# Grouping the value products of an attention kernel two blocks of keys at a time

## What is computed

```python
q, k = _apply_rope(q, cos, sin), _apply_rope(k, cos, sin)
scores = jnp.einsum('bhqd,bhkd->bhqk', q, k) / jnp.sqrt(jnp.float32(dh))
scores = jnp.where(causal[None, None, :, :], scores, -jnp.inf)
attn = jax.nn.softmax(scores, axis=-1)
out = jnp.einsum('bhqk,bhkd->bhqd', attn, v)
```

## Time and profile before

| | us |
|---|---|
| median of 3 runs (1317.09 to 1321.57) | 1317.52 |
| the profiled execution | 1314.68 |
| its span, first to last instruction | 1312.8 |
| TensorE busy | 1207.6 (92%) |
| VectorE busy | 732.1 (56%) |
| GpSimd busy | 696.6 (53%) |
| ScalarE busy | 486.5 (37%) |
| mean granted TensorE clock | 0.967 |

### The profile page before, as it was taken

How to read it: one execution, slowest core, us unless ns; L and a number is a source line. 1 busy time by engine, 2 the same in 40 slices (tenths; PEclk the granted TensorE clock), 3 DMA queues, 4 the chain that set the end, 5 groups by cost and what they waited for, 6 DMA issues and landing times.

```text
span 1312.8 us, 25609 instructions
## 1 busy us (share of the span) xinstructions
PE 1207.6 (92%) x8264; PEld 1000.3 (76%) x8264; DVE 732.1 (56%) x1512; ACT 486.5 (37%) x988; POOL 696.6 (53%) x984
## 2 busy tenths in 40 slices
PE   3799999999999999978999999999999999999950
PEld 3466666666666666568899999999999999999950
DVE  5777787878777876665334433343433334333554
ACT  2145454545454545533333323333322333322310
POOL 4234335353535351577567655576665566752675
PEclk9599999999999999989999999999999999999985
DMA  5776745454545455441321121131211222101366
GB/s 135 208 235 178 228 103 169 101 165 103 165 102 163 104 151 110 149 150 44 113 65 59 57 70 65 64 104 57 66 61 62 94 77 66 56 29 34 103 206 234
DMA packets 83100, 147.85 MB, mean 113 GB/s; under 512 B 9647, under 2 KB 60728, under 8 KB 78910
## 3 DMA queue, kind: packets, MB, share of 16 engines
q1 hardware_dynamic: 65344, 111.37, 29.7%
q0 software_dynamic: 7936, 26.60, 5.9%
q10 hardware_dynamic: 9728, 8.67, 2.1%
HBM read 93.05 MB, written 53.61 MB: 112 GB/s over the span
## 4 chain that ended last, share of the span: by engine, by line
PE 48%; POOL 1%; DVE 1%; issue 1%; DMA 0%; POOLq 0%; DVEq 0%
PE ps L77 47%; PE ps L1266 1%; DVE raw L1429 1%; POOL wf_hi L1546 1%; POOL wg_hi L1546 1%; DMA wg_hi<-slot_outputs,slot_all 0%; POOLq L1574 0%; POOL wp_lo L1546 0%; DVE al L1419 0%; DVE ah L1410 0%; DVE xl L1334 0%; DVEq L1574 0%; POOLq L1546 0%; DVE o_sb L1444 0%; DVE gated L1457 0%
## 5 line engine op out<-in xcount | busy, mean ns | idle before, releaser
L1493 POOL TENSOR_TENSOR al<-hid,ah 128x384 fp32r<-128x384 f32 (+1 forms) x176 | 187.4, 1065 | 232.7 <-DVE ah L1410 232.7
L1362 ACT ACTIVATE fc<-ps,b_fc 128x384 f32<-128x384 f32 (+1 forms) x192 | 115.6, 602 | 451.1 <-PE ps L77 451.1
L1457 DVE SCALAR_TENSOR_TENSOR gated<-ps,b_gate,fc 128x384 f32<-128x384 f32 (+1 forms) x192 | 123.4, 642 | 236.9 <-PE ps L77 226.4
L796 DVE TENSOR_REDUCE mx<-ps 128x2 f32<-128x256 f32 (+3 forms) x256 | 205.7, 818 | 39.0 <-PE ps L411 37.5
L411 PE MATMUL ps<-kst,qst 65*128 65x256 f32 (+2 forms) x512 | 149.8, 376 | 0.0
L579 ACT ACTIVATE probs<-ps 128x512 f32<-128x512 f32 (+1 forms) x256 | 125.3, 542 | 60.8 <-PE ps L437 59.8
L1444 DVE TENSOR_TENSOR o_sb<-ps,b_proj 128x256 f32<-128x256 f32 x80 | 33.9, 424 | 176.5 <-PE ps L77 176.5
L571 ACT ACTIVATE probs<-ps 128x256 f32<-128x256 f32 (+1 forms) x128 | 62.6, 490 | 151.6 <-PE ps L428 151.1
L937 POOL TENSOR_TENSOR rope_c<-qk_b,rope_table 128x512 f32<-128x512 f32 x32 | 42.6, 1330 | 128.1 <-ACT qk_b L607 128.0
L77 PE MATMUL ps<-xl,wg_hi 128*128 128x384 f32 (+1 forms) x384 | 103.1, 350 | 1.7 <-issue 1.7
L437 PE MATMUL ps<-qst,kst 66*128 66x512 f32 (+1 forms) x256 | 103.5, 448 | 0.0
(11 more groups left out here) (181 smaller groups left out, 2540.0 us busy)
## 6 DMA issues: line engine op xcount, KB each, us to landing
qk_parts<-hilo SPq DMA_DIRECT2D x32, 512.0 KB, 2.8
qst<-qk_parts SPq DMA_DIRECT2D x64, 256.0 KB, 4.8
kst<-qk_parts SPq DMA_DIRECT2D x64, 256.0 KB, 5.2
slot_tokens<-zeros POOLq DMA_DIRECT2D x12, 816.0 KB, 6.4
rows<-slot_tokens SPq DMA_DIRECT2D x24, 384.0 KB, 3.8
slot_outputs<-o_sb SPq DMA_DIRECT2D x72, 128.0 KB, 1.7
raw<-in_wf SPq DMA_DIRECT2D x8, 1024.0 KB, 5.2
raw<-in_wg SPq DMA_DIRECT2D x8, 1024.0 KB, 7.4
```

What stands on the lines that cost most here:

```text
L796: V.reduce_max(mx[:, g % 2, 2 * pr:2 * pr + 2, i], both[:, :, 0:P * (i + 1)], AXX)\
L1362: A(fc[:, hc % 2, 0:width], ps[:, FC + hc % 2, 0:width], ACT.Identity, bias=b_fc[:, e, hc:hc + 1]).then_inc(fc_out, 1)
L1457: V.scalar_tensor_tensor(gated[:, hc % 2, 0:width], ps[:, GATE + hc % 2, 0:width], b_gate[:, e, hc:hc + 1], fc[:, hc % 2, 0:width], ALU.ad ...
L1493: G.tensor_tensor(al[:, at, 0:width], hid[:, hc % 2, 0:width], ah[:, at, 0:width].bitcast(F32), ALU.subtract).then_inc(al_done, 1)
```

## The change

The tile of probabilities with two buffers becomes four tiles, one for each block of keys, each as wide as that block's queries. In slot 5 the value products of blocks 0 and 1 follow one another, in slot 1 of the next step those of blocks 2 and 3. ScalarE's wait before it writes block j is now for the product of block j of the step before.

```diff
-        probs = sb("probs", [P, 2, GH, T])
+        probs = [sb(f"probs{j}", [P, GH, T - P * j]) for j in range(TT)]
...
-                    last = mm(pvb[32 * h:32 * h + 32, P * j:T], v_sb[:, j, GH * g + h, :], probs[:, j % 2, h, P * j:T],
+                    last = mm(pvb[32 * h:32 * h + 32, P * j:T], v_sb[:, j, GH * g + h, :], probs[j][:, h, :],
                               start=(j == 0), stop=(j == TT - 1))
...
-                        if u in (3, 5, 7) and (not isinstance(b, int) or 0 <= s - 2 <= 31):
-                            pv(s - 2, b - (g < 2), (g - 2) % 4, (u - 3) // 2)
+                        if u == 5 and (not isinstance(b, int) or 0 <= s - 2 <= 31):
+                            pv(s - 2, b - (g < 2), (g - 2) % 4, 0)
+                            pv(s - 2, b - (g < 2), (g - 2) % 4, 1)
                         if u == 1 and (not isinstance(b, int) or 0 <= s - 3 <= 31):
+                            pv(s - 3, b - (g < 3), (g - 3) % 4, 2)
                             pv(s - 3, b - (g < 3), (g - 3) % 4, 3)
...
-                        wait(act, pv_done, 4 * t + j - 1)
-                    A(probs[:, j % 2, 2 * pr:2 * pr + 2, P * j:T],
+                        wait(act, pv_done, 4 * t + j - 3)
+                    A(probs[j][:, 2 * pr:2 * pr + 2, :],
...
-                        wait(act, pv_done, 4 * t + j - 1)
-                    A(probs[:, j % 2, 2 * pr + hh, P * j:T], ps[:, S2 + hh, P * j - q0:T - q0], ACT.Exp,
+                        wait(act, pv_done, 4 * t + j - 3)
+                    A(probs[j][:, 2 * pr + hh, :], ps[:, S2 + hh, P * j - q0:T - q0], ACT.Exp,
```

## The result

The changed kernel takes 1333.34 us (1331.37 to 1334.00, 4 runs), the kernel before 1317.3 in the same comparison: ratio 1.0113, 95% interval 1.0088 to 1.0137. It is slower, as forecast. It lies within the range for 8 in 10 (1312 to 1335), just outside the forecast's own (1321 to 1333), and 6 us above the number: 16 us more than before, where 9.5 were forecast. The profiled execution has a span of 1329.5 us for 1312.8, at a mean granted clock of 0.955 for 0.967.

A forecast was written before the change was run, and what follows sets the result against it. TensorE was taken to bound the attention loop; +8.5 us for batches 2 to 6, +1.0 for batch 1 and 0 for the outer batches gave +9.5, a median of 1327.0 us (own range 1321 to 1333, 8 in 10: 1312 to 1335).

The forecast's parts named there:

- the joins: Two value groups run together, sparing a change of array shape: 0.18 us each, 0.36 a step, 11.4 over 32 steps.
- Rival (d): At the pairs, joining saves nothing because the array empties between accumulations anyway: 11.4 us not saved, 1338 us; chance 0.04.
- Tiles, waits, ScalarE at nothing: Probability tiles (20 KB a partition for 16), looser waits and ScalarE's exponentials add 0, at most 0.1 us a batch either way.
- The cover: Value groups leaving slots 3 and 7 had filled TensorE's waits for VectorE; moving them makes a loop batch 1.7 us longer.
- the four waits: New TensorE waits: 0.7 us at xn's second transposes, 0.9 step 1's projection, about 2 step 2's slot 4, 0.9 the maxima.
- the walk: Following TensorE's lateness slot by slot through one loop batch's four steps: +1.7 us a batch, 8.5 for batches 2 to 6.
- the 0.66 of slot 7: Time freed when the third value group leaves slot 7, 0.66 us; at the maxima it gains nothing before step 3.
- Rival (a): In the attention loop cover doesn't matter, only saved shape changes count: -11.4 us, 1306.1 us; chance 0.13.
- Rival (b): Losses at the projection (0.82) and the maxima (0.66) are half as large: +5.3 us, 1323 us; chance 0.16.
- the 0.82 of the walk: Loss at step 1's slot 4 projection, which waits for VectorE's division: -0.24 instead of -1.06, 0.82 us, six times.
- The lock: VectorE and GpSimd share ports exclusively; 1.85 us of the copy of v waits for GpSimd's addition, order kept.
- Rival (c): The copy of v goes before GpSimd's addition; six batches give back 1.85 us each, 11.1 us: -1.6, 1316 us; chance 0.09.

The follow-up runs named there:

- 11: Changed kernel with the first pair behind slot 3's attention transposes (slot 5 in step 0), the second in slot 0 before the maxima's transpose: 1310.7 us, ratio 0.9949.
- experiment 1: Changed kernel's four tiles and looser ScalarE waits, but all value products in their old slots as in the kernel before: 1318.3 us, ratio 1.0008.
- experiment 3: Changed kernel with only the second pair joined (blocks 2 and 3 in slot 1), blocks 0 and 1 alone in slots 3 and 5: 1323.5 us, ratio 1.0044.
- 2: Changed kernel with only the first pair joined (blocks 0 and 1 in slot 5), block 2 in slot 7, block 3 in slot 1: 1327.7 us, ratio 1.0068.
- experiment 5: Changed kernel with 20 extra matmuls, result thrown away, in TensorE's wait at slot 4 of step 2: 1331.8 us, ratio 1.0105.
- 8: Changed kernel with GpSimd's addition of bias to residual waiting until VectorE's copy of v is done: 1335.5 us, ratio 1.0125.
- experiment 9: Kernel before with GpSimd's addition of bias to residual waiting until VectorE's copy of v is done: 1322.1 us, ratio 1.0033.
- experiment 6: Changed kernel with GpSimd's addition moved from slot 1 to slot 7 of step 2, away from the copy of v: 1341.3 us, ratio 1.0174.
- 7: Kernel before with GpSimd's addition moved from slot 1 to slot 7 of step 2, away from the copy of v: 1345.6 us, ratio 1.0216.
- experiment 4: Changed kernel, but in step 2 block 0 stays in slot 3 and block 1 stands alone in slot 5: 1326.7 us, ratio 1.0044.
- 12: Kernel of 11 with GpSimd's addition also waiting until VectorE's copy of v is done: 1312.4 us, ratio 0.9961.

## Why the prediction was right, and where its size was off

**Bound and saving.** TensorE was the bound, and the joins save what was worked out and a little more. A joined pair lasts 1.64 us against 1.00 + 0.78 and one entry of 0.09, so each join gives 0.23, not 0.18. With the pairs at better places (11) the saving reaches the time: 1.3 us a batch less, though step 2 gains nothing. Rival (d), a join that saves nothing, is out.

**Tiles, waits, ScalarE at nothing.** Shown by experiment 1.

**The cover.** Each of the four waits appeared where the walk had put it, and each half of the change costs by itself (3 at full clock, 2 with part of its price in clock). The walk's +1.7 us a batch is met by the +1.6 of the one batch in experiment 5 at full clock. It is met step by step too: from one transpose of the maxima to the next the walk comes to 0.0, +0.5, +1.6 and -0.4 us for the four steps (with the 0.66 of slot 7 taken off at the end of step 1), and that batch has -0.3, +0.5, +1.6 and -0.2 against batch 6 of before. Rival (a), that cover does not matter, fell with experiment 3: a saved join and still 0.8 us a batch more. Rival (b), half of two losses, would have given 1.0 us a batch for the whole order (1.7 less 0.41 and 0.33); at the projection it was partly right, since the wait there is 0.63 us for the 0.82 of the walk.

**The lock.** The order of addition and copy stayed (2.54 us again in the changed kernel). Rival (c) assumed that 1.85 us come free if the copy goes first. Experiments 8 and 9 show that with routing instructions behind the copy they don't, they pass on to one of those; the chain gets shorter only where none stands there (batch 1) or with the addition far away (6 and 7). The rule of the Trainium skill (page "SBUF — State Buffer", section "SBUF: two separate sides"), an exclusive lock held for a whole instruction, fits both: 2.54 us behind the addition before, 2.23 now. What failed was my reading that it concerns the copy alone.

**What was missed.** The sum had no term for the clock, and took the durations at full speed for granted. The addition over the changed kernel: the order costs 5 x 67.83 - 331.45 = 7.7 us in batches 2 to 6, 0.5 in batch 1 (64.2 at full clock in experiment 5, 63.7 before) and -0.2 in batch 7, together 8.0 of the forecast 9.5. Batches 2 to 6 take 346.35 us together for 331.45, 14.9 more, of which 7.7 is order; the other 7.2 I put down to the clock, as all of it lies in step 2. Batch 1 takes 66.6, 2.4 more than at full clock. So the clock costs 9.6 us in the loop and batch 1, by a price for the order that comes from one batch. Before batch 1 the kernel is 2.3 us ahead (93.8 for 96.0), behind batch 8's first maxima 1.4 behind. Neither is the change's doing as far as is shown: batch 0 had a mean clock of 0.92 for 0.86, and the last part takes 768.3 to 774.1 us in the profiles of all these kernels, which hardly differ there. 8.0 + 9.6 - 2.3 + 1.4 = 16.7, which is what the span grew by.

So direction and mechanism were foreseen, and the clock's 9.6 us were not. That the time is inside the stated range is in part luck: the range was wide enough for a term that it didn't know.

**What stays open.** Why the clock falls in one batch and not in the next with the same waits (experiments 4 and 5) isn't settled. Stands of 0.96 and 0.76 us in one step passed at full clock in every batch of experiment 3, and the same two were followed by a low clock in four of five batches of the loop in experiment 4, which has the 0.63 of the projection besides. That the stands bring it about is supported by its moving from behind the one to behind the other when the first was filled; it isn't shown for a single stand. Over batches 2 to 6 of the profiles, each batch with 2.2 us or more at slot 4 of step 2 had a low stretch (the changed kernel, experiments 2 and 8), two of five with 1.5 us (12), one of five with 1.3 (9), and none with 0.9 to 1.0 in the kernel before and in experiments 1, 3 and 11; but experiment 4 had four with 0.96, behind the later stand. The rival that all waits of a stretch count together, whichever is the longest, was named before experiment 6 and isn't excluded, since the addition's new place made a longer stand of its own.

## What to carry to other kernels

A group of instructions that can be moved is also the cover for whatever its engine would otherwise wait for; before it is moved, list at its old place which waits come next and how far ahead their releasers are, and put it down again in front of such a wait. The same two joins cost 1.1% at one place and gain 0.5% at another. And where TensorE runs nearly without gaps, a new stand can cost as much again in clock as in waiting, here 9.6 us beside 8.0.

## What the runs showed of the hardware that was not expected

- TensorE's granted clock, 1.00 (2.4 GHz) through the loop before, fell to 0.5 (1.2 GHz) for part of each of batches 1 to 6 of the changed kernel, at the stand of 2.46 us or just behind it. Where the low stretch lay behind the maxima, a batch with a mean of 0.98 took 1.6 us longer than the same at 1.00, one with 0.95 3.3 us (experiment 5). In the changed kernel, where it lay behind the long stand in step 2, the same means cost 0.9 to 1.3 and 2.0 to 2.2 us.
- Filling that stand with 2.35 us of matmuls moved the fall in four batches of six, to behind the next stand, and removed it in two (experiment 5).
- GpSimd's addition over two tiles of 1024 elements a row holds up a VectorE instruction of 8 elements a row (2.23 us for 0.23), one that takes a value for each row from a second tile, while the one with constants alone that began together with the addition took 0.17 us. Putting one VectorE instruction ahead of the addition gained nothing where such an instruction followed (step 2 18.0 us for 17.8), and 1.1 us where none did (15.9 for 17.0, batch 1; experiment 9).
